# First block of the second feed-forward product: a first group cut in four, and the token tiles interleaved chunk by chunk

## The chip, the cores and the metric

The kernel runs on one core of one Trainium2 chip. The metric is the device time of the whole program in microseconds (us), lower is better. TensorE (PE in the rows) does the matrix products, VectorE (DVE) and ScalarE (ACT) the elementwise work, GpSimd (POOL) small operations and stores, SyncE (SP) issues loads.

## The reference, cut to what matters

A decoder layer with three parts, each followed by a layer norm: causal self-attention sums, a cross-attention with a bias, and a quantised feed-forward network. Only the last product of the network is touched.

```
def _L0_ffn_ref(x, W_in, b_in, W_out, b_out):
    W_in_sim = quantize_w8_per(W_in, axis=0)
    W_out_sim = quantize_w8_per(W_out, axis=1)      # one scale per row (per hidden unit)
    x_sim = quantize_a16(x)                         # one scale for the whole tensor
    hidden = jax.nn.gelu(x_sim @ W_in_sim + b_in, approximate=False)   # (8192 tokens, 2048)
    hidden_sim = quantize_a16(hidden)               # needs max |hidden| over everything
    out = hidden_sim @ W_out_sim + b_out            # (8192, 2048) @ (2048, 512)
    return out
x = _layernorm(x + ffn(x), axis=-1)
```

Because `quantize_a16` of the hidden values needs the maximum over all of them, the second product cannot begin before the first one has ended everywhere.

## The kernel before, in words

The 8192 tokens are worked in 16 blocks (`NBLK`) of 512 tokens (`BLK`), each block in four tiles of 128 tokens (t = 0..3). The 2048 hidden units are 16 chunks of 128 (`FC`, index f); four chunks are a group (`FG` = 4 groups, index g or f // 4). The first product writes its results to a table in memory; the last stage, which is the one changed, reads them back.

In this last stage one group of one block is a tile of 128 x 2048 numbers (4 chunks x 512 tokens), and it passes through five steps:

- `load_group` (SP, L1771) loads it as `hT`.
- `shift` (ACT, L1825) scales it and adds a rounding constant, into `g32`. The rows call this buffer `bt_main`, whose memory it uses.
- `scale_rows` (DVE, L1878) takes the constant off and multiplies by one number per chunk, in four instructions of 128 x 512.
- `high` (ACT, L1833) copies it to 16 bits, `g_hi`.
- `low` (DVE, L1887) writes the rest, `g_lo`. With this the group is ready for TensorE, and `lo_ready` counts it.

TensorE (`blk`, L1951) then computes for every tile t the sum over 16 chunks of two matmuls (`g_hi`, `g_lo`) each: 32 matmuls in one accumulator bank, `ps[t]`. It waits on `lo_ready` only in tile 0, at chunks 0, 4, 8 and 12, since the later tiles read the same groups. The last matmul of a tile counts `o_done`.

VectorE then finishes the tile. `residual` (L1897 to L1905) adds the residual to `ps[t]` and takes mean and variance, GpSimd computes the root (L1800), and `finish` (L1913) writes the normalised tile, which GpSimd stores.

All engines run in the order in which their instructions stand. On VectorE the order for block n is written out by hand; it works on the output tile t of block n and on group t of block n + 1 in turn:

```
for t in range(4):
    scale_rows(n + 1, t)
    residual(n, t)          # waits on o_done for tile t of block n
    low(n + 1, 1 - e, t)
    finish(n, t)            # waits for the root from GpSimd
```

Only for block 0 a prologue makes the four groups ahead of that loop. The names of the counters are `shifted` (after `shift`), `g_ready` (after `scale_rows`), `hi_ready` (after `high`) and `lo_ready` (after `low`).

Of the kernel before, what the change touches and what calls it, by code (L numbers as in the profile page):

```python
# [15 lines left out]
ALU = mybir.AluOpType  # L16
ACT = mybir.ActivationFunctionType
# [3 lines left out]
P = 128  # L21
# [1317 lines left out]
def feed_forward_stage(nc, x2_rows, w_in_rows, b_in, w_out_rows, b_out, hidden, resid, out, block, sems, shared, tail):  # L1339
# [3 lines left out]
    FC = FF // P  # L1343
    FG = FC // 4
    ROUND = 1.5 * 2.0 ** 23
# [5 lines left out]
    with ExitStack() as outer:  # L1351
# [3 lines left out]
        w2 = keep("w2", [P, FC, DIM], F16)  # L1355
        row_scale = keep("row_scale", [P, FC], F32)
# [3 lines left out]
        hT = keep("hT4", [P, FG, 4, BLK], F32)  # L1360
        hT_in = [sems.enter_context(nc.semaphore(f"hT_in{g}")) for g in range(FG)]
# [359 lines left out]
        with ExitStack() as ctx:  # L1721
# [9 lines left out]
            h_scale = sb("h_scale", [P, 1], F32)  # L1731
            o_scale = sb("o_scale", [P, 1], F32)
            minus_half = sb("minus_half4", [P, 1], F32)
            round_c = sb("round_c", [P, 1], F32)
# [5 lines left out]
            g_hi = sb("g_hi", [P, 2, FC, BLK], F16)  # L1740
            g_lo = sb("g_lo", [P, 2, FC, BLK], F16)
# [3 lines left out]
            g32 = shared.bt_main  # L1745
            ps = [ctx.enter_context(nc.psum_tensor(f"ps4{i}", [P, DIM], F32)) for i in range(4)]
# [18 lines left out]
            @block.sync  # L1765
            def _(sp):
                def load_group(n, g):
                    if not (isinstance(n, int) and n == 0):
                        sp.wait_ge(shifted, 4 * n + g - 3)
                    src = hidden[n:n + 1] if isinstance(n, int) else hidden[bass.ds(n, 1)]  # L1770
                    sp.dma_start(hT[:, g], src[:, g].rearrange("n p c t -> p (n c) t")).then_inc(hT_in[g], 16)  # L1771

                def load_row(n, t):
                    if not (isinstance(n, int) and n == 0 and t < 2):
                        sp.wait_ge(y_ready, 4 * n + t - 1)
                    src = resid[n:n + 1] if isinstance(n, int) else resid[bass.ds(n, 1)]
                    sp.dma_start(xrb[:, t % 2], src[:, :, t, :].rearrange("n p d -> p (n d)")).then_inc(xrb_in[t % 2], 16)

                for g in range(FG):
                    sp.wait_ge(h_out[g], 16 * NBLK)  # L1780
                sp.wait_ge(xres_out, 16 * NBLK)
                for g in range(FG):
                    load_group(1, g)
                    load_row(0, g)
                for n in range(1, NBLK - 1):
                    for g in range(FG):
                        load_group(n + 1, g)
                        load_row(n, g)
                for g in range(FG):
                    load_row(NBLK - 1, g)  # L1790
# [26 lines left out]
            @block.scalar  # L1817
            def _(act):
                def shift(n, g):

                    k = 4 * n + g
                    act.wait_ge(hT_in[g], 16 * (n + 1))
                    if not (isinstance(n, int) and n == 0):
                        act.wait_ge(lo_ready, k - 3)
                    act.activation(g32[:, g], hT[:, g], ACT.Identity, bias=round_c[:],  # L1825
                                   scale=h_scale[:]).then_inc(shifted, 1)

                def high(n, e, g):
                    k = 4 * n + g
                    act.wait_ge(g_ready, k + 1)  # L1830
                    if g == 0 and not (isinstance(n, int) and n < 2):
                        act.wait_ge(o_done, 4 * (n - 1))
                    act.activation(g_hi[:, e, 4 * g:4 * g + 4, :], g32[:, g], ACT.Copy).then_inc(hi_ready, 1)  # L1833

                act.wait_ge(scale_step, 3)
                act.wait_ge(round_set, 1)
                shift(0, 0)

                def blk(n, e):
                    for g in range(FG):  # L1840
                        if g < 3:
                            shift(n, g + 1)
                        elif not (isinstance(n, int) and n == NBLK - 1):
                            shift(n + 1, 0)
                        high(n, e, g)

                blk(0, 0)
                blk(1, 1)
                for m in range(1, NBLK // 2 - 1):
                    blk(2 * m, 0)  # L1850
                    blk(2 * m + 1, 1)
                blk(NBLK - 2, 0)
                blk(NBLK - 1, 1)

            @block.vector
            def _(dve):
# [16 lines left out]
                def scale_rows(n, g):  # L1873

                    k = 4 * n + g
                    dve.wait_ge(shifted, k + 1)
                    for c in range(4):
                        ins = dve.tensor_scalar(g32[:, g, c, :], g32[:, g, c, :], ROUND,  # L1878
                                                row_scale[:, 4 * g + c:4 * g + c + 1], ALU.subtract, ALU.mult)
                    ins.then_inc(g_ready, 1)  # L1880

                def low(n, e, g):
                    k = 4 * n + g
                    dve.wait_ge(hi_ready, k + 1)
                    if g == 0 and not (isinstance(n, int) and n < 2):
                        dve.wait_ge(o_done, 4 * (n - 1))
                    dve.tensor_tensor(g_lo[:, e, 4 * g:4 * g + 4, :], g32[:, g], g_hi[:, e, 4 * g:4 * g + 4, :],  # L1887
                                      ALU.subtract).then_inc(lo_ready, 1)
# [26 lines left out]

                for g in range(FG):
                    dve.wait_ge(h_out[g], 16 * NBLK)
                scale_rows(0, 0)
                for g in range(FG):
                    if g + 1 < FG:  # L1920
                        scale_rows(0, g + 1)
                    low(0, 0, g)

                def blk(n, e):
# [16 lines left out]
            @block.tensor  # L1941
            def _(pe):
                def blk(n, e):
                    for t in range(4):
                        if not (isinstance(n, int) and n == 0):
                            pe.wait_ge(y_ready, 4 * n + t - 3)
                        for f in range(FC):
                            if t == 0 and f % 4 == 0:
                                pe.wait_ge(lo_ready, 4 * n + f // 4 + 1)
                            for a, g in enumerate((g_hi, g_lo)):  # L1950
                                mm = pe.matmul(ps[t][:], g[:, e, f, t * P:(t + 1) * P], w2[:, f, :],  # L1951
                                               start=(f == 0 and a == 0), stop=(f == FC - 1 and a == 1))
                        mm.then_inc(o_done, 1)

                blk(0, 0)
                blk(1, 1)
                for m in range(1, NBLK // 2 - 1):
                    blk(2 * m, 0)
                    blk(2 * m + 1, 1)
                blk(NBLK - 2, 0)  # L1960
                blk(NBLK - 1, 1)
# [112 lines left out]
```

## Time and profile before

| | us |
|---|---|
| median of 3 runs | 2286.9 |
| lowest and highest of them | 2265.87, 2289.72 |
| the profiled execution | 2284.26 |
| its span in the trace | 2282.5 |
| TensorE busy | 2111.4 (93% of the span) |
| VectorE busy | 1735.8 (76%) |
| ScalarE busy | 1082.4 (47%) |
| granted TensorE clock, mean | 0.955 of 2.4 GHz |

Times in the rows are counted from the start of the span. The last stage begins at about 1805 us, when the first product has ended, and reaches to the end of the span. A row of the timeline gives start, duration, engine, line, operation, the tile written and the tiles read, and in brackets how long the engine had been idle and what ended that.

### The profile page before, as it was taken

The page shows a single profiled execution, that of the slowest core. Times are in us where ns is not written, and L with a number is a line of the kernel's source. Part 1 is how long each engine was busy: PE and PEld are TensorE (multiplying, and loading weights), DVE is VectorE, ACT ScalarE, POOL GpSimd, SP SyncE. Part 2 cuts the span into 40 slices and gives each one's busy share as a digit, 9 for nine tenths or more (in the row PEclk, how much of TensorE's full clock was granted, in tenths as well). Part 3 has the DMA queues.
Part 4 walks back from the last instruction along what each step waited for, and adds up shares of the span by engine and source line. Part 5 has one row for each costly group of instructions (what it writes and reads, how often), then busy time and mean ns, then how long its engine had stood idle before and what let it go on. Part 6 is the DMA issues. An engine that isn't in the chain of part 4 may idle for free.

```text
span 2282.5 us, 32943 instructions
## 1 busy us (share of the span) xinstructions
PE 2111.4 (93%) x11904; PEld 1167.9 (51%) x11904; DVE 1735.8 (76%) x3296; ACT 1082.4 (47%) x1522; POOL 822.0 (36%) x802
## 2 busy tenths in 40 slices
PE   7999999984798998999999859999999699999997
PEld 3444444431586776777777524444444344444443
DVE  6768686865677897898898656777666488888885
ACT  1444444443444555555555224444444565555551
POOL 2122221222125555556455432222222134444442
PEclk9999999996779999999999779999999899999999
DMA  6334243457749969979975437888888656666662
GB/s 233 108 126 155 94 148 110 115 137 176 188 128 208 260 166 191 279 183 208 262 181 153 136 84 267 288 288 289 267 270 272 249 195 227 224 233 230 226 226 79
DMA packets 386626, 448.46 MB, mean 196 GB/s; under 512 B 279270, under 2 KB 279430, under 8 KB 368032
## 3 DMA queue, kind: packets, MB, share of 16 engines
q1 hardware_dynamic: 322448, 286.07, 46.0%
q0 software_dynamic: 64016, 160.28, 22.9%
q8 instruction: 95, 1.56, 0.3%
q14 instruction: 67, 0.55, 0.1%
HBM read 258.93 MB, written 138.73 MB: 174 GB/s over the span
## 4 chain that ended last, share of the span: by engine, by line
PE 82%; DVE 7%; issue 6%; ACT 1%; DMA 1%; POOL 1%; SPq 0%; DVEq 0%; POOLq 0%; ACTq 0%
PE ps_h L1708 19%; PE ps L1951 19%; PE ps_proj L600 10%; PE ps_o L1275 8%; PE ps_w L1304 7%; PE ps_s L620 5%; PE ps_m L1227 3%; PE ps_o L1271 3%; PE ps_m L1229 3%; PE ps_l L1253 3%; DVE rope_t L428 1%; PE ps_t L1289 1%; PE ps_l L1250 1%; DVE x_hi L411 1%; DVE stack L1099 1%
## 5 line engine op out<-in xcount | busy, mean ns | idle before, releaser
L1708 PE MATMUL ps_h<-xT,b_rows 128*128 128x512 f16 x2048 | 444.7, 381 | 13.1 <-DMA xT<-x_lo 13.1
L1951 PE MATMUL ps<-w,g_hi 128*128 128x512 f16 x1024 | 389.3, 380 | 21.1 <-DVE g_lo L1887 21.1
L1951 PE MATMUL ps<-w,g_lo 128*128 128x512 f16 x1024 | 389.1, 380 | 0.0
L1708 PEld LDWEIGHTS ps_h<-xT,b_rows 128*128 128x128 f16 x2048 | 200.9, 98 | 256.6 <-issue 16.6
L1549 ACT ACTIVATE h<-ps_h,b_rows 128x512 f32<-128x512 f32 x256 | 199.0, 777 | 241.5 <-PE ps_h L1708 241.5
L1275 PEld LDWEIGHTS ps_o<-vm,pT 128*128 128x128 f32 x2048 | 299.2, 202 | 13.0
L1099 DVE TENSOR_REDUCE stack<-ps_m 128x2 f16<-128x308 f32 x512 | 244.2, 479 | 55.3 <-PE ps_m L1229 53.6
L1275 PE MATMUL ps_o<-vm,pT 128*128 128x33 f32 x2048 | 284.8, 265 | 0.0
L1050 ACT ACTIVATE pT<-logit 128x512 f32<-128x512 f32 x320 | 199.0, 624 | 132.3 <-DVE logit L1117 131.4
L1622 DVE TENSOR_REDUCE amax_t<-h 128x1 f32<-128x2048 f32 x64 | 146.2, 2284 | 120.8 <-ACT h L1549 120.8
L1800 POOL TENSOR_TENSOR rstd<-vare,minus_half 128x1 f32<-128x1 f32 x64 | 152.3, 2380 | 208.5 <-DVE vare L1905 208.5
L1833 ACT ACTIVATE g_hi<-bt_main 128x2048 f16<-128x2048 f32 x64 | 122.2, 1909 | 179.0 <-DVE bt_main L1878 179.0
L969 POOL TENSOR_TENSOR comb_lo<-comb,comb_hi 128x512 f16<-128x512 f32 x64 | 74.0, 1157 | 347.6 <-ACT comb_hi L1059 347.6
L1227 PE MATMUL ps_m<-kb,q_heads 128*128 128x308 f16 x512 | 161.6, 316 | 35.1 <-DVE stack L1099 15.3
L309 ACT ACTIVATE raw<-ps_proj 128x512 bf16<-128x512 f32 x128 | 76.4, 597 | 231.0 <-PE ps_proj L600 231.0
L1304 PE MATMUL ps_w<-wo_hi,combT 128*128 128x512 f16 x512 | 161.0, 398 | 24.3 <-DVE y L1145 20.8
L1117 DVE TENSOR_TENSOR logit<-ps_l,bt_main 128x512 f32<-128x512 f32 x256 | 174.0, 681 | 3.6 <-PE ps_l L1253 3.5
L1951 PEld LDWEIGHTS ps<-w,g_hi 128*128 128x128 f16 x1024 | 100.4, 98 | 144.4 <-DVE g_lo L1887 23.5
L1951 PEld LDWEIGHTS ps<-w,g_lo 128*128 128x128 f16 x1024 | 100.4, 98 | 120.8 <-issue 0.8
L1229 PE MATMUL ps_m<-b_rows,ident_h 128*128 128x308 f16 x512 | 161.3, 315 | 0.0
L1502 POOL DMA_DIRECT2D hidden<-h x64 | 35.7, 558 | 322.0 <-ACT h L1549 322.0
L1887 DVE TENSOR_TENSOR g_lo<-bt_main,g_hi 128x2048 f16<-128x2048 f32 x64 | 146.2, 2285 | 1.9 <-ACT g_hi L1833 1.5
(182 smaller groups left out, 3840.1 us busy)
## 6 DMA issues: line engine op xcount, KB each, us to landing
hidden<-h POOLq DMA_DIRECT2D x64, 1024.0 KB, 6.7
hT<-hidden SPq DMA_DIRECT2D x64, 1024.0 KB, 6.2
xc<-x_cols SPq DMA_DIRECT2D x16, 1024.0 KB, 5.1
xr<-x_rows SPq DMA_DIRECT2D x16, 1024.0 KB, 5.5
x_rows<-x POOLq DMA_DIRECT2D x16, 1024.0 KB, 4.8
x1t<-x_rows SPq DMA_DIRECT2D x64, 256.0 KB, 3.8
bt_main<-bias_main SPq DMA_DIRECT2D x16, 1024.0 KB, 6.3
xres<-x_rows SPq DMA_DIRECT2D x64, 256.0 KB, 4.1
```

Of the source, the lines that this page charges most:

```text
L600: mm = pe.matmul(ps_proj[job % 2][:], w[:, m, c, o * P:(o + 1) * P], x_[:, j % 2, c, :], start=(s == 0), stop=(s == len(terms) - 1))
L1050: act.activation(pT[:, g % 2, k, :], logit[:, (g + k) % 4], ACT.Exp, scale=SCALE).then_inc(exp_done, 1)
L1099: dve.tensor_reduce(stack[:, tile % 3, 2 * k:2 * k + 2, 3 * HD], ps_m[k % 2][:, 0:2 * KEYS].rearrange("p (h k) -> p h k", h=2), AX.X, ALU. ...
L1117: dve.tensor_tensor(logit[:, (g + k) % 4], ps_l[(5 * g + k) % 2][:], bias, ALU.add).then_inc(biased, 1)
L1227: pe.matmul(out, q_heads[:, t % 2, (k // 2) * P:(k // 2 + 1) * P], kb[:, eu, 2 * k * KEYS:(2 * k + 2) * KEYS], start=True, stop=False)
L1229: pe.matmul(out, ident_h[:], b_rows[:, t, 2 * k:2 * k + 2, :], start=False, stop=True).then_inc(mx_done, 1)
L1275: mm = pe.matmul(ps_o[c][:, base + h * VW:base + (h + 1) * VW], pT[:, g % 2, part, tok], vm[:, eu, 4 * g + h, :], start=False, stop=(part ...
L1304: mm = pe.matmul(ps_w[:], combT[:, eu, a, c, t * P:(t + 1) * P], w[:, c, :], start=(c == 0 and a == 0 and w is wo_hi), stop=(c == KC - 1 a ...
L1549: act.activation(h[:, f // 4, f % 4, :], ps_h[f % 4][:], ACT.Gelu, bias=b_in_sb[:, f:f + 1], scale=col_scale[:, f:f + 1]).then_inc(h_ready, 1)
L1708: mm = pe.matmul(ps_h[f % 4][:], w1[:, c, f * P:(f + 1) * P], xT[:, e, a, :, c, :], start=(a == 0 and c == 0), stop=(a == 1 and c == KC - 1))
L1800: pool.tensor_tensor(rstd[:, s:s + 1], vare[:, s:s + 1], minus_half[:], ALU.pow).then_inc(rstd_ready, 1)
L1951: mm = pe.matmul(ps[t][:], g[:, e, f, t * P:(t + 1) * P], w2[:, f, :], start=(f == 0 and a == 0), stop=(f == FC - 1 and a == 1))
```

## The change

The first group of block 0 passes through ScalarE and VectorE in four pieces of one chunk (128 x 512) and not as a whole. TensorE works block 0 with the chunk as its outer loop and the four token tiles as its inner one, so that each chunk is used for all four tiles before the next is taken. The counters of all later groups are shifted by three, because the first group now counts four times. The loops `blk` of all engines for blocks 1 to 15 are otherwise as they were; on VectorE this includes the loop that is quoted above for n = 0.

```
@@ SyncE, load_group
-                        sp.wait_ge(shifted, 4 * n + g - 3)
+                        sp.wait_ge(shifted, 4 * n + g)
@@ ScalarE, shift and high
-                        act.wait_ge(lo_ready, k - 3)
+                        act.wait_ge(lo_ready, k)
-                    act.wait_ge(g_ready, k + 1)
+                    act.wait_ge(g_ready, k + 4)
@@ ScalarE
-                shift(0, 0)
+                def shift_piece(c):
+                    act.activation(g32[:, 0, c], hT[:, 0, c], ACT.Identity, bias=round_c[:],
+                                   scale=h_scale[:]).then_inc(shifted, 1)
+                def high_piece(c):
+                    act.wait_ge(g_ready, c + 1)
+                    act.activation(g_hi[:, 0, c, :], g32[:, 0, c], ACT.Copy).then_inc(hi_ready, 1)
+                act.wait_ge(hT_in[0], 16)
+                shift_piece(0)
+                for c in range(4):
+                    if c < 3:
+                        shift_piece(c + 1)
+                    high_piece(c)
                 def blk(n, e):
                     for g in range(FG):
+                        if n == 0 and g == 0:
+                            shift(0, 1)
+                            continue
                         if g < 3:
                             shift(n, g + 1)
@@ VectorE, scale_rows and low
-                    dve.wait_ge(shifted, k + 1)
+                    dve.wait_ge(shifted, k + 4)
-                    dve.wait_ge(hi_ready, k + 1)
+                    dve.wait_ge(hi_ready, k + 4)
@@ VectorE
-                scale_rows(0, 0)
-                for g in range(FG):
-                    if g + 1 < FG:
-                        scale_rows(0, g + 1)
+                def scale_piece(c):
+                    dve.wait_ge(shifted, c + 1)
+                    dve.tensor_scalar(g32[:, 0, c, :], g32[:, 0, c, :], ROUND, row_scale[:, c:c + 1],
+                                      ALU.subtract, ALU.mult).then_inc(g_ready, 1)
+                def low_piece(c):
+                    dve.wait_ge(hi_ready, c + 1)
+                    dve.tensor_tensor(g_lo[:, 0, c, :], g32[:, 0, c], g_hi[:, 0, c, :], ALU.subtract).then_inc(lo_ready, 1)
+                scale_piece(0)
+                for c in range(4):
+                    if c < 3:
+                        scale_piece(c + 1)
+                    low_piece(c)
+                for g in range(1, FG):
+                    scale_rows(0, g)
                     low(0, 0, g)
@@ TensorE
-                                pe.wait_ge(lo_ready, 4 * n + f // 4 + 1)
+                                pe.wait_ge(lo_ready, 4 * n + f // 4 + 4)
-                blk(0, 0)
+                def first_blk():
+                    for f in range(FC):
+                        if f < 4:
+                            pe.wait_ge(lo_ready, f + 1)
+                        elif f % 4 == 0:
+                            pe.wait_ge(lo_ready, f // 4 + 4)
+                        for t in range(4):
+                            for a, g in enumerate((g_hi, g_lo)):
+                                mm = pe.matmul(ps[t][:], g[:, 0, f, t * P:(t + 1) * P], w2[:, f, :],
+                                               start=(f == 0 and a == 0), stop=(f == FC - 1 and a == 1))
+                            if f == FC - 1:
+                                mm.then_inc(o_done, 1)
+                first_blk()
```

On TensorE, at the beginning of block 0, the bank names change (`ps40` to `ps43` are the four tiles). Before:

```order
L1951 MATMUL ps40<-w2,g_hi 128x512 [waits lo_ready]
L1951 MATMUL ps40<-w2,g_lo 128x512
L1951 MATMUL ps40<-w2,g_hi 128x512
L1951 MATMUL ps40<-w2,g_lo 128x512
L1951 MATMUL ps40<-w2,g_hi 128x512
L1951 MATMUL ps40<-w2,g_lo 128x512
```

And in the changed kernel:

```order
L1994 MATMUL ps40<-w2,g_hi 128x512 [waits lo_ready]
L1994 MATMUL ps40<-w2,g_lo 128x512
L1994 MATMUL ps41<-w2,g_hi 128x512
L1994 MATMUL ps41<-w2,g_lo 128x512
L1994 MATMUL ps42<-w2,g_hi 128x512
L1994 MATMUL ps42<-w2,g_lo 128x512
L1994 MATMUL ps43<-w2,g_hi 128x512
L1994 MATMUL ps43<-w2,g_lo 128x512
L1994 MATMUL ps40<-w2,g_hi 128x512 [waits lo_ready]
```

A chunk now serves eight matmuls in four banks, where it served two in one. At the end of block 0 and the beginning of block 1 TensorE has, in the changed kernel:

```order
L1994 MATMUL ps40<-w2,g_hi 128x512
L1994 MATMUL ps40<-w2,g_lo 128x512
L1994 MATMUL ps41<-w2,g_hi 128x512
L1994 MATMUL ps41<-w2,g_lo 128x512
L1994 MATMUL ps42<-w2,g_hi 128x512
L1994 MATMUL ps42<-w2,g_lo 128x512
L1994 MATMUL ps43<-w2,g_hi 128x512
L1994 MATMUL ps43<-w2,g_lo 128x512
L1981 MATMUL ps40<-w2,g_hi 128x512 [waits lo_ready,y_ready4]
```

Before, the last matmul of `ps40` stood 96 matmuls ahead of that last row; now it stands 7 ahead of it. On VectorE, from the first group of block 0 to the first tile, the order before was:

```order
L1878 TENSOR_SCALAR bt_main<-bt_main,row_scale 128x512 x3
L1878 TENSOR_SCALAR bt_main<-bt_main,row_scale 128x512 [waits shifted]
L1878 TENSOR_SCALAR bt_main<-bt_main,row_scale 128x512 x3
L1887 TENSOR_TENSOR g_lo<-bt_main,g_hi 128x2048 [waits hi_ready]
L1878 TENSOR_SCALAR bt_main<-bt_main,row_scale 128x512 [waits shifted]
L1878 TENSOR_SCALAR bt_main<-bt_main,row_scale 128x512 x3
L1887 TENSOR_TENSOR g_lo<-bt_main,g_hi 128x2048 [waits hi_ready]
```

And in the changed kernel (L1938 and L1943 are the pieces):

```order
L1938 TENSOR_SCALAR bt_main<-bt_main,row_scale 128x512 [waits shifted]
L1943 TENSOR_TENSOR g_lo<-bt_main,g_hi 128x512 [waits hi_ready]
L1938 TENSOR_SCALAR bt_main<-bt_main,row_scale 128x512 [waits shifted]
L1943 TENSOR_TENSOR g_lo<-bt_main,g_hi 128x512 [waits hi_ready] x2
L1895 TENSOR_SCALAR bt_main<-bt_main,row_scale 128x512 [waits shifted]
L1895 TENSOR_SCALAR bt_main<-bt_main,row_scale 128x512 x3
L1904 TENSOR_TENSOR g_lo<-bt_main,g_hi 128x2048 [waits hi_ready]
L1895 TENSOR_SCALAR bt_main<-bt_main,row_scale 128x512 [waits shifted]
L1895 TENSOR_SCALAR bt_main<-bt_main,row_scale 128x512 x3
L1904 TENSOR_TENSOR g_lo<-bt_main,g_hi 128x2048 [waits hi_ready]
```

The scaling of a later group used to stand ahead of the `low` of the group before it; now `low` comes first, and the scaling of groups 2 and 3 stands behind it.

## Rows read from the trace of the kernel before

**Rows 1.** The page's chain that ended last, its shares by engine

```profile
PE 82%; DVE 7%; issue 6%; ACT 1%; DMA 1%; POOL 1%; SPq 0%; DVEq 0%; POOLq 0%; ACTq 0%
```

**Rows 2.** The same chain in order of time, around block 0: start, us, what

```profile
1813.98 4.08 ACT bt_main L1825 x2
...
1831.24 2.30 DVE g_lo L1887
...
1833.60 66.43 PE ps L1951 x307
```

**Rows 3.** Windows: busy us per engine, then granted clock, DMA share, GB/s

```profile
1822.20:1825.60 3.40, 3.36 (x8) 1.04 (x8) 3.40 (x5) 3.40 (x3) 0.00 (x0) 0.50 1.03 417
...
1826.00:1829.80 3.80, 2.00 (x8) 0.72 (x8) 3.75 (x5) 3.80 (x3) 0.00 (x0) 0.97 0.23 97
...
1856.00:1883.70 27.70, 27.70 (x130) 12.56 (x129) 24.47 (x45) 15.62 (x9) 12.61 (x8) 1.00 0.68 226
```

**Rows 4.** Timeline of TensorE in block 0

```profile
1822.24 0.61 PE L1951 MATMUL ps<-w,g_hi 128*128 128x512 f16 x1 [17.23 <-DVE g_lo L1887]
...
1825.20 0.63 PE L1951 MATMUL ps<-w,g_lo 128*128 128x512 f16 x1
1826.02 0.49 PE L1951 MATMUL ps<-w,g_hi 128*128 128x512 f16 x1 [0.19 <-DVE g_lo L1887]
...
1833.60 0.39 PE L1951 MATMUL ps<-w,g_hi 128*128 128x512 f16 x1 [1.89 <-DVE g_lo L1887]
...
1835.12 0.38 PE L1951 MATMUL ps<-w,g_lo 128*128 128x512 f16 x1
...
1848.93 0.38 PE L1951 MATMUL ps<-w,g_lo 128*128 128x512 f16 x1
```

**Rows 5.** Timeline of ScalarE in block 0

```profile
1817.96 1.89 ACT L1833 ACTIVATE g_hi<-bt_main 128x2048 f16<-128x2048 f32 x1
1819.76 2.08 ACT L1825 ACTIVATE bt_main<-hT,round_c,h_scale 128x2048 f32<-128x2048 f32 x1
1821.75 1.89 ACT L1833 ACTIVATE g_hi<-bt_main 128x2048 f16<-128x2048 f32 x1
```

**Rows 6.** Timeline of VectorE: output tiles 0 and 3 of block 0

```profile
1835.53 0.75 DVE L1897 SCALAR_TENSOR_TENSOR y<-ps,o_scale,xrb 128x512 f32<-128x512 f32 x1 [0.41 <-PE ps L1951]
...
1837.34 2.28 DVE L1887 TENSOR_TENSOR g_lo<-bt_main,g_hi 128x2048 f16<-128x2048 f32 x1
...
1856.25 0.75 DVE L1897 SCALAR_TENSOR_TENSOR y<-ps,o_scale,xrb 128x512 f32<-128x512 f32 x1 [0.23 <-PE ps L1951]
...
1858.06 2.28 DVE L1887 TENSOR_TENSOR g_lo<-bt_main,g_hi 128x2048 f16<-128x2048 f32 x1
...
1861.26 1.67 DVE L1878 TENSOR_SCALAR bt_main<-bt_main,row_scale 128x512 f32<-128x512 f32 x4
1863.16 0.75 DVE L1897 SCALAR_TENSOR_TENSOR y<-ps,o_scale,xrb 128x512 f32<-128x512 f32 x1 [0.23 <-PE ps L1951]
```

**Rows 7.** Groups by shape with 128x512 operands: count, busy us, mean ns

```profile
L1549 ACT ACTIVATE h<-ps_h,b_rows 128x512 f32<-128x512 f32 x256 | 199.0, 777 | 241.5 <-PE ps_h L1708 241.5
L1059 ACT ACTIVATE comb_hi<-comb 128x512 f16<-128x512 f32 x64 | 39.3, 614 | 6.2 <-DVE comb L1132 6.2
L1117 DVE TENSOR_TENSOR logit<-ps_l,bt_main 128x512 f32<-128x512 f32 x256 | 174.0, 681 | 3.6 <-PE ps_l L1253 3.5
L1878 DVE TENSOR_SCALAR bt_main<-bt_main,row_scale 128x512 f32<-128x512 f32 x256 | 106.9, 480 | 1.9 <-ACT bt_main L1825 1.9
```

**Rows 8.** Windows around two waits of TensorE in the cross-attention stage

```profile
732.70:735.30 2.60, 0.01 (x1) 0.00 (x0) 0.76 (x2) 1.54 (x2) 0.18 (x1) 1.00 1.03 395
...
888.00:893.36 5.36, 0.01 (x2) 0.03 (x2) 0.81 (x2) 1.54 (x2) 1.32 (x2) 0.78 1.41 246
893.36:895.00 1.64, 1.62 (x4) 0.38 (x5) 1.56 (x6) 0.00 (x0) 0.00 (x0) 0.50 1.75 193
...
897.00:899.00 2.00, 2.00 (x12) 1.49 (x11) 1.87 (x4) 1.08 (x3) 0.00 (x0) 0.79 1.31 96
```

## The prediction

> **What bounds the kernel now.** I read the chain of work that ended last first. TensorE holds 82% of it [rows 1], and in the last stage it is the only link from 1833.60 us on [rows 2]. The windows then say what a full stretch of that stage looks like: from 1856.00 to 1883.70 TensorE is busy all of 27.70 us at a granted clock of 1.00, which is the higher level, 2.4 GHz, with VectorE busy 24.47 us beside it [rows 3]. So a later block is bound by TensorE, with VectorE close behind. The beginning of the stage is the exception: ScalarE and VectorE prepare the first groups while TensorE waits, 17.23 us before its first matmul and 1.89 us before the last of the four groups [rows 4].
>
> From the timeline of TensorE come two durations. At the higher level 71 matmuls lie between the starts 1833.60 and 1848.93, which makes 0.216 us each, so 1.73 for the 8 matmuls that tile 0 has for one group and 6.91 for the 32 of a tile. At the lower level (1.2 GHz, 0.50 in [rows 3]) the first eight start 0.423 us apart, 1822.24 to 1825.20 [rows 4]. After 1833.60 tile 0 has 8 matmuls left and the other tiles 96. Block 0 thus ends at 1833.60 + 104 x 0.216 = 1856.06, and block 1, with 128, at 1883.71, if nothing waits. Nothing does [rows 3].
>
> **Part 1, the four pieces.** The trace has no such pieces, so I take the nearest 128x512 shapes: 0.78 us for ScalarE with bias and scale, 0.61 for its copy, 0.68 for a VectorE subtraction, 0.48 for the scaling by a chunk's number [rows 7]. ScalarE's next instruction starts about 0.09 before the one ahead ends (1.89 long, next after 1.80; 2.08 long, next after 1.99) [rows 5]. From ScalarE's start at 1813.98 [rows 2]: first shift to 1814.76, second to 1815.45, first copy (the first scaling, to 1815.3, is done) to 1815.97, first subtraction to about 1816.7. TensorE's first matmul is then at 1816.8, where it was at 1822.24: 5.4 us earlier.
>
> The price is on ScalarE. Four shifts and four copies take 4 x (0.69 + 0.52) = 4.84 us, where one of each took 1.99 + 1.80 = 3.79. Moreover the second group's shift no longer stands ahead of the first group's copy. ScalarE comes to it at 1818.9 (the fourth copy waits for a scaling), ends it at 1821.0 and the third group's at 1823.0. The scaling of group 1 ends at 1822.7, its copy at 1824.8, its subtraction at 1827.1. The scaling of group 2 now stands behind that subtraction, so a group costs 1.67 + 1.91 + 2.28 = 5.86 in series: groups 2 and 3 are ready at about 1833 and 1839.
>
> The Trainium skill ("VectorE: DVE Perf Modes", section on the TRN2 errata) speaks against such pieces: instructions on on-chip memory pay a fixed part each. The rows show it at the size used above, and by an estimate from the page's ScalarE figure the six added instructions would cost 1.1 us, against the 1.05 above, so the sum would be the same.
>
> **Part 2, four tiles per chunk.** A chunk now feeds 8 matmuls and a group 32, 6.91 us, more than the 5.86 that the next group needs. So TensorE starts at 1816.8, runs 3.8 us (9 matmuls) at the lower level as it did before, does the other 23 of the group to 1825.5, waits to 1827.15 for group 1, and then does 96 without a wait: 1827.15 + 20.74 = 1847.9. Group 2 is wanted at 1834.1 and group 3 at 1841.0, so these have 1 and 2 us to spare. **Block 0 ends 8.2 us earlier.** Bounds: with group 1 there in time 1846.2 (9.9 earlier); with group 1 a further microsecond late 7.2.
>
> **Part 3, what stands behind block 0.** This is what decides. VectorE's loop for block 0 is unchanged: scaling of group t of block 1, residual of tile t of block 0, `low` of group t of block 1, `finish` of tile t. Before, tile 0 was complete at 1835.5, and during tiles 1 to 3 VectorE had 20 us in which it could make `low` of block 1, one group per tile; the last ended at 1858.06 + 2.28 = 1860.34 and was wanted at 1856.06 + 24 x 0.216 = 1861.24 [rows 6]. It was made just in time. Now all four tiles end together: `ps40` ends 7 matmuls before the end of the block. Behind the residual of tile 0, on VectorE, stands everything that block 1 needs, and TensorE waits for it at once, since its tile 0 wants all four groups.
>
> Working: the last matmul of tile 0 starts at 1847.9 - 7 x 0.216 = 1846.4. The residual starts 0.41 later (1835.12 to 1835.53 [rows 4, 6]), `low` 1.81 after it, and takes 2.28 [rows 6], and TensorE starts 0.06 behind its end (1831.24 + 2.30 to 1833.60 [rows 2]): 1846.8 + 1.81 + 2.28 + 0.06 = 1850.95. **That is a wait of 3.05 us.** Then each further group costs VectorE a whole turn of its loop. A turn is 1863.16 - 1856.25 = 6.91 us, 0.23 of it waiting for TensorE [rows 6], so 6.68 when the tiles are there; in it TensorE has only 8 matmuls, 1.73. Three turns are three waits of 4.95, **14.85 us**. Group 3 of block 1 reaches TensorE at 1850.95 + 20.04 = 1871.0, and the block ends at 1871.0 + 22.46 = 1893.5, where it ended at 1883.7: **9.7 us later**. Nothing gives this back, since from there on TensorE is the bound.
>
> ScalarE's copies of block 1 lie beside the residuals (1.91 in 1.81) and add 0.1 at most per turn. Loads: `hT` of group 3 of block 1 stands on SyncE behind a load that waits for the first residual; it is used two turns later. Both cost nothing, and with a short turn that cover would go.
>
> **The clock.** After a wait of 2.6 us the clock was still at 1.00. In one of 5.36 us it fell (mean 0.78), then stood at 0.50 with TensorE busy to about 897.8, 4.5 us [rows 8]. At the beginning of the stage it was low for 3.8 us [rows 3, 4]. The waits of 4.95 lie nearer to the 5.36. In the first groups the lower level hides in the waits (3.4 us of work in a turn of 6.68). Behind the last one it counts, half of 3.8 to 4.5 us: **2.0 us**. Bounds: 0, if the bursts keep the level or raise it before the last, and 4.4, if it lasts twice as long.
>
> The Trainium skill ("TensorE: Matmul & The Clock Gate", section "HAM oscillation — how this bites in real kernels") has the case of bursts with waits between them, each of which starts at the lower clock. By it the term stands as taken; without it the sum would be 2.0 less.
>
> **The sum.** -8.2 + 3.05 + 14.85 + 2.0 = +11.7 us. Against the profiled execution, 2284.26 (span 2282.5 and 1.8 around it), that makes 2296.0. The median shown is 2.6 above that execution, so I forecast 2286.9 + 11.7 = 2298.6. About 1% (22.9 us) is what a measurement of this kernel can tell from no change: its three runs lie 24 us apart.
>
> **Rivals.**
>
> A, not slower: the wait in block 1 doesn't come, and block 0's gain stays: 2286.9 - 8.2 = 2278.7. The Trainium skill ("Perfetto Trace Analysis", section on optimizing Scalar/DVE operations) has it so: breaking up instructions may let waiting engines go on sooner, which holds of part 1. It decides at the turn L for which 3.05 + 3 x (L - 1.73) = 8.2, L = 3.4 us. Against it: scaling, residual's first instruction and `low` alone are 1.67 + 0.75 + 2.28 = 4.70 [rows 6]. Chance 0.05.
>
> B, slower by over 1%: the clock stays low behind the last wait. At 0.423 - 0.216 = 0.207 us for each matmul, it takes 64 matmuls at the lower level (22.9 - 9.7 = 13.2) to pass the bound; all 104 would give 2286.9 + 9.7 + 21.5 = 2318. Against it: in both places the clock rose after 3.8 to 4.5 us of work [rows 4, 8]. Chance 0.05.
>
> C, the change doesn't do what it says in block 0: ScalarE and VectorE are later by over 2 us per group than worked out, and TensorE waits for groups 2 and 3 as before. The gain goes, the wait of block 1 stays: up to +19.9, 2306.8. Against it: 5.86 against 6.91 per group. Chance 0.06.
>
> D, VectorE stays behind: after group 3 it comes 2.6 to the residual of tile 0 of block 1, which TensorE has ended after 2.0, so it is 0.6 behind. It gains 0.23 a tile, and `low` of the next block has 0.9 to spare, so I count nothing. If that isn't so, a few more waits come, 1 to 4 us: 2299.6 to 2302.6. Chance 0.10.
>
> The forecast has 0.74. The range, 2276 to 2309, takes in A, C and D and the bounds of the terms, and at its lower end a median out of runs such as the lowest one (2265.87 + 11.7 = 2277.6). Slower by over 1% needs 2309.8: B and, by the scatter of the runs, some of C and of the forecast, 0.13. Faster by over 1% needs less than 2264: 0.03. Within 1%: 0.84.
>
> **What would show it.** First matmul of block 0 near 1816.8, one wait of about 1.7 before its group 1, end near 1848. Then waits of TensorE on VectorE's `low`: one of 3 and three of about 5 us (less by 1.7 where the clock is at 0.50), 24 matmuls of tile 0 of block 1 spread over 20 us, and from block 2 on no wait. VectorE has no idle time ahead of the residuals of tiles 1 to 3 of block 0. The prediction is wrong if the turn is much shorter than 6.7, or if block 1's groups are ready ahead of the first residual.

## The result

The changed kernel takes 2288.86 us in the median of 20 runs, the kernel before 2277.86 in 20. The ratio is 1.0049, with a 95% interval of 1.0027 to 1.0072: slower by about 11 us, which is less than the 1% bound and clear of zero. One of the 20 runs of the kernel before took 2766 us; the ratio leaves it out. Forecast were +11.7 us. The median itself lies 9.7 below the forecast one, since that was counted from 2286.9, and the median of the kernel before came out 9.0 lower with more runs.

The profiled execution of the changed kernel has a span of 2282.6 us, the one before 2282.5. That doesn't contradict the ratio. The two executions differ ahead of the change: the last stage of the changed one happened to begin 10.8 us earlier, and its first product had already begun 10.6 us earlier (1349.72 against 1360.28). So I measure the **length of the last stage**, from ScalarE's first shift to the end of the span. It is 2282.5 - 1813.98 = 468.5 us before [rows 2] and 2282.6 - 1803.15 = 479.45 after, **+10.9**. All times called "after the shift" below count from that first shift.

The chain of the changed kernel in order of time (start, us, what). It answers to [rows 2]:

```profile
1803.15 1.52 ACT bt_main L1839 x2
...
1814.17 2.30 DVE g_lo L1904
...
1816.52 19.61 PE ps L1994 x90
1836.15 0.76 DVE y L1914
...
1838.20 2.51 POOL rstd L1800
...
1841.19 1.74 DVE bt_main L1895 x4
1842.96 1.92 ACT g_hi L1833
...
1857.52 2.30 DVE g_lo L1904
1859.82 0.05 issue
1859.87 40.33 PE ps L1981 x179
```

Before, TensorE held the chain from 1833.60, 19.6 us after the shift, to the end. Now it holds it from 1816.52, loses it at 1836.15 to VectorE, GpSimd and ScalarE for three turns of a loop, and has it back for good only at 1859.87, 56.7 us after the shift.

TensorE's timeline: the rows at which a wait ends, and the first row behind the last wait that is at the higher clock level again. They answer to [rows 4]:

```profile
1806.03 0.61 PE L1994 MATMUL ps<-w,g_hi 128*128 128x512 f16 x1 [11.83 <-DVE g_lo L1943]
...
1816.52 0.39 PE L1994 MATMUL ps<-w,g_hi 128*128 128x512 f16 x1 [0.58 <-DVE g_lo L1904]
...
1840.38 0.38 PE L1981 MATMUL ps<-w,g_hi 128*128 128x512 f16 x1 [2.98 <-DVE g_lo L1904]
...
1847.25 0.61 PE L1981 MATMUL ps<-w,g_hi 128*128 128x512 f16 x1 [4.98 <-DVE g_lo L1904]
...
1853.56 0.61 PE L1981 MATMUL ps<-w,g_hi 128*128 128x512 f16 x1 [2.72 <-DVE g_lo L1904]
...
1859.87 0.61 PE L1981 MATMUL ps<-w,g_hi 128*128 128x512 f16 x1 [2.71 <-DVE g_lo L1904]
...
1863.13 0.38 PE L1981 MATMUL ps<-w,g_hi 128*128 128x512 f16 x1
```

Block 0 has 96 matmuls from 1816.52 on and ends at 1837.26, 34.1 after the shift (42.1 before): 8.0 us gained. Block 1 then has 3.12 us to its first matmul and turns of 6.87, 6.31 and 6.31 us with 8 matmuls each. From 1863.13 it runs 96 without a wait to 1883.87, 80.7 after the shift (69.7 before): 11.0 us lost. The stage's +10.9 is all there; later blocks give nothing back and cost nothing.

VectorE's timeline shows the loop that sets these turns. It answers to [rows 6]:

```profile
1836.15 0.75 DVE L1914 SCALAR_TENSOR_TENSOR y<-ps,o_scale,xrb 128x512 f32<-128x512 f32 x1 [6.40 <-PE ps L1994]
...
1837.96 2.28 DVE L1904 TENSOR_TENSOR g_lo<-bt_main,g_hi 128x2048 f16<-128x2048 f32 x1
1840.73 0.55 DVE L1930 TENSOR_SCALAR o<-y,mv,rstd 128x512 f32<-128x512 f32 x1 [0.49 <-POOL rstd L1800]
1841.19 1.73 DVE L1895 TENSOR_SCALAR bt_main<-bt_main,row_scale 128x512 f32<-128x512 f32 x4
1842.85 0.74 DVE L1914 SCALAR_TENSOR_TENSOR y<-ps,o_scale,xrb 128x512 f32<-128x512 f32 x1
...
1844.90 2.29 DVE L1904 TENSOR_TENSOR g_lo<-bt_main,g_hi 128x2048 f16<-128x2048 f32 x1 [0.18 <-ACT g_hi L1833]
1847.11 0.54 DVE L1930 TENSOR_SCALAR o<-y,mv,rstd 128x512 f32<-128x512 f32 x1
```

VectorE stood idle 6.40 us ahead of the first residual, waiting for the end of block 0, with the groups of block 1 behind it in its queue. After that it is idle only for 0.49 us (the root) and 0.18 us (ScalarE's copy) in the first turn, and for 0.18 us in each of the next two.

Windows of the changed kernel (busy per engine, granted clock, DMA share, GB/s), to be set against [rows 3, 8]:

```profile
1837.30:1840.38 3.08, 0.11 (x1) 0.03 (x1) 2.86 (x5) 0.00 (x0) 2.18 (x1) 1.00 0.82 192
1840.38:1842.10 1.72, 1.72 (x8) 0.68 (x8) 1.37 (x4) 0.00 (x0) 0.84 (x2) 1.00 0.93 391
1842.10:1847.25 5.15, 0.17 (x1) 0.01 (x1) 4.86 (x9) 3.90 (x2) 0.79 (x2) 0.87 0.66 191
1847.25:1850.60 3.35, 3.35 (x8) 1.03 (x8) 3.32 (x7) 1.33 (x1) 0.62 (x1) 0.50 0.67 269
...
1862.80:1890.00 27.20, 27.20 (x127) 12.37 (x126) 23.70 (x43) 14.67 (x8) 12.61 (x8) 1.00 0.63 218
```

The wait of 3 us left the clock up, the one of 5 let it fall. The second, third and fourth bursts ran at 0.50, and 8 matmuls of the fourth cost 1.5 us more than at the higher level.

### The profile page after: what moved, and what is told of

Read it like the earlier page. It is cut to its first block, busy times and chain, and to the rows that moved or that the text cites. A ratio compares the mean times of both kernels' runs of the same rounds, so it can differ in the third digit from the quotient of the medians.

```text
span 2282.6 us, 32952 instructions
## 1 busy us (share of the span) xinstructions
PE 2113.2 (93%) x11904; PEld 1165.6 (51%) x11904; DVE 1734.8 (76%) x3299; ACT 1083.9 (47%) x1528; POOL 822.5 (36%) x802
## 4 chain that ended last, share of the span: by engine, by line
PE 82%; DVE 7%; issue 5%; ACT 2%; DMA 1%; POOL 1%; SPq 0%; DVEq 0%; POOLq 0%; ACTq 0%
PE ps_h L1708 19%; PE ps L1981 18%; PE ps_proj L600 10%; PE ps_o L1275 8%; PE ps_w L1304 7%; PE ps_s L620 5%; PE ps_m L1227 3%; PE ps_o L1271 3%; PE ps_m L1229 3%; PE ps_l L1253 3%; DVE rope_t L428 1%; PE ps_t L1289 1%; PE ps L1994 1%; PE ps_l L1250 1%; DVE x_hi L411 1%
## 5 line engine op out<-in xcount | busy, mean ns | idle before, releaser
L1981 PE MATMUL ps<-w,g_hi 128*128 128x512 f16 x960 | 366.8, 382 | 13.4 <-DVE g_lo L1904 13.4
L1981 PE MATMUL ps<-w,g_lo 128*128 128x512 f16 x960 | 366.7, 382 | 0.0
L1981 PEld LDWEIGHTS ps<-w,g_hi 128*128 128x128 f16 x960 | 94.5, 98 | 130.5 <-DVE g_lo L1904 12.7
L1981 PEld LDWEIGHTS ps<-w,g_lo 128*128 128x128 f16 x960 | 94.5, 98 | 114.2 <-issue 2.5
```

## The experiments

The table gives the stage length by the trace, and the timed ratio to the kernel before where there is one. Where the clock behaves alike, the stage length repeats within 0.1 us (479.45 and 479.4 for the changed kernel); the kernel before has one profile.

| | stage, us | against before | timed ratio (95% interval) |
|---|---|---|---|
| before | 468.5 | | |
| changed | 479.45 | +10.9 | 1.0049 (1.0027 to 1.0072) |
| e1 pieces only | 475.6 | +7.1 | 1.0047 (1.0012 to 1.0082) |
| e2 chunks only | 483.0 | +14.5 | 1.0125 (1.0086 to 1.0163) |
| e3 changed, filler in the waits | 478.0 | +9.5 | |
| e4 changed, block 1's groups first | 472.1 | +3.6 | 1.0054 (1.0022 to 1.0087) |
| e5 tiles in pairs | 472.1 | +3.6 | 1.0034 (1.0004 to 1.0064) |
| e6 as e4, lighter block 0 | 472.1 | +3.6 | |
| e7 changed, prologue pipelined | 480.9 | +12.4 | |
| e8 as e4, earlier loads | 471.4 | +2.9 | |
| e9 as e8, lighter block 0 | 468.6 | +0.1 | |
| e10 as e8, finishes put off | 470.85 | +2.3 | 1.0005 (0.9979 to 1.0031) |
| e11 changed, again | 479.4 | +10.9 | |
| e12 as e7, again | 479.5 | +10.9 | |

In e2 and e4 the timed ratios say more than the stage: about 28 and 12 us, with intervals that begin at 20 and 5 us, against 14.5 and 3.6. These are 4 and 10 runs whose earlier stages scatter too. Where the difference comes from isn't shown, and the text below rests on the stage.

**e1, one half alone: the pieces.** In the changed kernel TensorE's first block gets its old loop order:

```
 def first_blk():
-    for f in range(FC):
-        ... waits on lo_ready at f
-        for t in range(4):
+    for t in range(4):
+        for f in range(FC):
+            ... the same waits, at t == 0
```

> The four pieces alone; TensorE works block 0 tile by tile as before. The measure is the length of the last stage, from ScalarE's first shift to the end of the span: 468.5 us before, 479.5 in the changed kernel. Theory (the waits stand in block 1, because all four tiles of block 0 end together): they don't come here, since tile 0 ends 20 us before the block. But tile 0 wants all four groups at once, and group 3 is ready 25.0 us after the first shift (it was 19.6), so block 0 ends at 25.1 + 22.5 = 47.6 where it was 42.1: stage +5.5 us, no wait in block 1. Rival (the pieces and the serial prologue are the whole loss): the stage is 11 us longer here as well. Rival (only the tile order matters): +0.

Measured: +7.1. No wait in block 1. Group 3 of block 0 reaches TensorE 25.06 after the shift, where it did at 19.62: +5.4. The rest is the clock, which I had not put in: the waits in tile 0 became longer (6.15, 2.26 and 2.56 us), it fell, and 8 matmuls behind the last one cost 1.7 us. The row of that last wait is

```profile
1828.08 0.39 PE L1993 MATMUL ps<-w,g_hi 128*128 128x512 f16 x1 [2.56 <-DVE g_lo L1904]
```

So this half alone is a loss, and in another way than the changed kernel: group 3 is late. Under the old order this is on the path, under the new one it is not. The pieces themselves are the smaller part of the delay. e7 has the pieces with the old prologue, and there group 3 is ready 20.9 us after the shift, 1.3 later than in the kernel before (19.6). The other 4.1 us belong to the serial prologue that e1 kept.

**e2, the other half: four tiles per chunk.** The kernel before, with TensorE's `blk(0, 0)` replaced:

```
-                blk(0, 0)
+                for f in range(FC):
+                    if f % 4 == 0:
+                        pe.wait_ge(lo_ready, f // 4 + 1)
+                    for t in range(4):
+                        ... two matmuls into ps[t]
```

> Four tiles per chunk in block 0 alone, without the pieces and with the old prologue. Theory: TensorE starts 8.3 us after the first shift, has the first group's 32 matmuls done at about 18 (13 of them at the lower clock level) and block 0 at 38.5, 3.6 us earlier than before; then the same waits come as in the changed kernel, 3 + 5 + 2.7 + 2.7 us of it seen at either clock level, block 1 takes 46.6 us in place of 27.65 (+19.0): stage +15 us, so this half alone is slower than both halves together. Rival (pieces are the loss): stage shorter than before, -3.6.

Measured: +14.5. TensorE has the same four waits, 2.98, 4.98, 2.72 and 2.71 us, only 3.6 us later than in the changed kernel. The two rows at the head of block 1:

```profile
1858.25 0.38 PE L1951 MATMUL ps<-w,g_hi 128*128 128x512 f16 x1 [2.98 <-DVE g_lo L1887]
1865.12 0.61 PE L1951 MATMUL ps<-w,g_hi 128*128 128x512 f16 x1 [4.98 <-DVE g_lo L1887]
```

The loss comes with this half. With it, the pieces are worth 3.6 us, since TensorE can use an early chunk at once. Block 0 ended 37.7 us after the shift and not at the expected 38.5, with 9 matmuls at the lower clock level and not 13.

**e3, the price of the clock.** In the changed kernel, for block 1, tile 0:

```
+                                if isinstance(n, int) and n == 1 and f > 0:
+                                    for _ in range(18):
+                                        pe.matmul(ps_fill[:], w2[:, 0, 0:P], w2[:, 0, :], start=True, stop=True)
                                 pe.wait_ge(lo_ready, 4 * n + f // 4 + 4)
```

> The changed kernel with 18 matmuls into a spare bank ahead of each of the three later groups of tile 0 of block 1, in the time that TensorE waits there (18 x 0.216 = 3.9 us in a wait of 5). They are work that the result doesn't use. This prices the clock alone: the granted clock should stay at 1.00 through block 1, and the 7 to 8 matmuls that ran 0.21 us longer behind the last wait should run at 0.216: stage 1.5 us shorter than the 479.5 of the changed kernel, with VectorE's turns as they are. If the clock term is nothing: no difference. If TensorE's loads or the filler slow VectorE: longer.

Measured: 1.5 us shorter than the changed kernel. The groups reach TensorE at the same times to 0.02 us, and the clock stays up through the whole of tile 0:

```profile
1854.00:1874.00 20.00, 17.61 (x80) 7.53 (x81) 18.64 (x35) 11.90 (x6) 4.22 (x7) 1.00 0.72 251
```

Of the 10.9 us, 1.5 are the clock, and 9.4 the waits for VectorE less what block 0 gained.

**e4, another order on VectorE.** In the changed kernel, VectorE's block 0:

```
-                blk(0, 0)
+                scale_rows(1, 0)
+                scale_rows(1, 1)
+                low(1, 1, 0)
+                scale_rows(1, 2)
+                low(1, 1, 1)
+                residual(0, 0)
+                scale_rows(1, 3)
+                low(1, 1, 2)
+                finish(0, 0)
+                low(1, 1, 3)
+                for t in range(1, 4):
+                    residual(0, t)
+                    finish(0, t)
```

On SyncE groups 3 of block 1 and 0 of block 2 are loaded ahead of the rows for tiles 2 and 3, and the prologue on VectorE is that of the kernel before, as in e7.

> The changed kernel with VectorE's block 0 loop written in another order: the first two groups of block 1 are made before the residual of tile 0, the last two before the residual of tile 1, with the loads that these need issued earlier, and the scaling of groups 2 and 3 of block 0 ahead of the subtraction before it. Theory A (only the order of this one loop is wrong): the waits of block 1 shrink from 13.4 to about 3 us and nothing comes in their place: stage 8 to 11 us shorter than in the changed kernel, at or below the 468.5 of before. Theory B (VectorE has no slack in any block, so what is put off comes due in the next one): the waits of block 1 shrink as in A, but the residuals and finishes of tiles 1 to 3 now stand behind them, and TensorE waits some 10 to 12 us for the groups of block 2: stage about 6 us longer than before, 4 to 5 shorter than in the changed kernel.

Measured: +3.6, and neither theory in full. The waits of block 1 shrink to 1.02 and 0.76 us. In block 2 two new ones come:

```profile
1877.00 0.61 PE L2002 MATMUL ps<-w,g_hi 128*128 128x512 f16 x1 [3.18 <-DVE g_lo L1911]
1883.31 0.61 PE L2002 MATMUL ps<-w,g_hi 128*128 128x512 f16 x1 [3.08 <-DVE g_lo L1911]
```

That is what theory B says in kind, but 6.3 us in place of 10 to 12: the three finishes in a row cost less than a turn each. Behind VectorE stood something else too, on ScalarE:

```profile
1858.10 2.10 ACT L1832 ACTIVATE bt_main<-hT,round_c,h_scale 128x2048 f32<-128x2048 f32 x1 [13.33 <-DMA hT<-hidden]
```

The load of group 1 of block 2 stood on SyncE behind rows that wait for residuals. VectorE lost 1.87 us behind it.

**e5, a middle way.** The kernel before, with block 0 in pairs of tiles on TensorE:

```
-                blk(0, 0)
+                for pair in ((0, 1), (2, 3)):
+                    for f in range(FC):
+                        ... wait on lo_ready at f % 4 == 0 of the first pair
+                        for t in pair:
+                            ... two matmuls into ps[t]
```

> The kernel before with block 0 worked chunk by chunk for tiles 0 and 1 and then for tiles 2 and 3 (no pieces). TensorE has 16 matmuls per group (3.5 us) while ScalarE delivers one per 3.8, so block 0 ends about 5 us earlier than before, at 37 us after the first shift. Tiles 0 and 1 are complete at about 24, so VectorE can go on. Theory B: TensorE's lead is worth nothing, since VectorE's loop sets when group 3 of block 1 is ready (47.3 us as before): the 5 us come back as waits in block 1, stage 468.5 +- 1. Theory A: stage 4 to 5 us shorter than before.

Measured: +3.6, where I expected none. TensorE did come to block 1 ahead of VectorE, and the lead came back as one wait of 4.96 us for its last group:

```profile
1855.23 0.61 PE L1951 MATMUL ps<-w,g_hi 128*128 128x512 f16 x1 [4.96 <-DVE g_lo L1887]
```

That is 48.6 us after the shift. The 47.3 of my expectation was when TensorE took this group in the kernel before; ready it was at 46.4 (1858.06 + 2.28 + 0.06 [rows 6]). So it came 2.2 us later than before, and 1.4 of these cost time. The first residual is 2.3 later (23.8, before 21.6), since tile 0 ends with tile 1, and VectorE waits once more for tile 2, which ends with tile 3:

```profile
1844.23 0.75 DVE L1897 SCALAR_TENSOR_TENSOR y<-ps,o_scale,xrb 128x512 f32<-128x512 f32 x1 [0.73 <-PE ps L1962]
```

The clock fell in the wait of 4.96 us and 11 matmuls behind it ran at the lower level, 2.3 us. Theory B holds in kind. Its size left out both, the 1.4 and the 2.3.

**e6, less work for VectorE.** As e4, with `bn_stats` and `bn_aggr` of block 0 replaced by two memsets, so that block 0 is left without its mean and variance and only the time is of use:

> As e4, and the mean and variance of the four tiles of block 0 left out on VectorE (replaced by constants, 0.7 to 0.9 us less per tile, so about 3.4 us less work). Theory B (VectorE's total work is what TensorE waits for in block 2): the stage is about 3.5 us shorter than in e4, with the waits of block 2 shorter by as much. Theory A: no difference from e4, since its waits would not be there.

Measured: as long as e4 (472.07 and 472.14). Taken alone this speaks for theory A. The trace shows why it doesn't: VectorE came 2.8 us earlier to block 2 and stood there, waiting for ScalarE, which waited for the load:

```profile
1854.20 2.29 DVE L1911 TENSOR_TENSOR g_lo<-bt_main,g_hi 128x2048 f16<-128x2048 f32 x1 [4.44 <-ACT g_hi L1840]
...
1850.28 2.09 ACT L1832 ACTIVATE bt_main<-hT,round_c,h_scale 128x2048 f32<-128x2048 f32 x1 [13.82 <-DMA hT<-hidden]
```

The test was spoilt by my own order of loads, so e8 and e9 repeat it without that.

**e7, the serial prologue.** In the changed kernel `scale_rows(0, g + 1)` stands ahead of `low(0, 0, g)` again.

> The changed kernel with the prologue of block 0 on VectorE as it was before: the scaling of groups 2 and 3 ahead of the subtraction of the group before. Groups 2 and 3 get ready about 2 and 4 us earlier, but TensorE didn't wait for them. Theory (all is set by the end of block 0 on TensorE): only the 0.6 us wait for group 1 can change, stage 479.5 to 478.9. Rival (the serial prologue costs): 2 to 4 us shorter.

Measured: 1.5 us longer than the changed kernel, as neither said. The waits are the same to 0.01 us except the one of group 1. Group 3 of block 0 is ready 4.1 us earlier, as expected, and TensorE doesn't want it so early. Its `low` here, from 18.59 us after the shift, and in the changed kernel, from 22.73:

```profile
1835.17 2.29 DVE L1904 TENSOR_TENSOR g_lo<-bt_main,g_hi 128x2048 f16<-128x2048 f32 x1 [1.50 <-ACT g_hi L1833]
```

```profile
1825.88 2.29 DVE L1904 TENSOR_TENSOR g_lo<-bt_main,g_hi 128x2048 f16<-128x2048 f32 x1 [1.98 <-ACT g_hi L1833]
```

The difference of 1.5 us is the number of matmuls at the lower level behind the last wait (low matmuls below): 14 here, 8 there. Windows from the last wait on, of this kernel and of its repetition e12, both 6.70 us:

```profile
1873.30:1880.00 6.70, 6.70 (x18) 2.49 (x19) 4.94 (x11) 3.90 (x2) 1.71 (x2) 0.55 0.50 163
```

```profile
1881.80:1888.50 6.70, 6.70 (x25) 2.75 (x26) 5.13 (x11) 3.89 (x2) 1.93 (x2) 0.77 0.51 161
```

**e11 and e12, the same two kernels again.**

> The changed kernel once more, unaltered. In its first profile 8 matmuls behind the last wait of block 1 ran at the lower clock level (1.5 us); in the kernel with the pipelined prologue it were 14 (2.9 us), with the same waits to 0.01 us. If that difference is of the execution and not of the kernel, this profile shows the same waits (3.0, 5.0, 2.7, 2.7 us) and a number of low matmuls between 7 and 16, and a stage of 479.4 to 481.

> The kernel with the pipelined prologue once more. As for e11: the waits as in its first profile, the low matmuls behind the last of them 7 to 16, stage 479.4 to 481. If the prologue's order costs the 1.5 us, it shows 14 and 480.9 again.

Measured: 479.4 and 479.5, with 7 and 8 low matmuls. So the 1.5 us of e7 belong to that execution: the same kernel had 14 once and 8 once. The order of the prologue is worth nothing here, which the theory had said.

**e8, e4 with earlier loads.**

```
                 load_group(1, 3)
-                load_group(2, 0)
+                for g in range(FG):
+                    load_group(2, g)
                 load_row(0, 2)
```

> As e4, with the loads of all four groups of block 2 issued ahead of the rows that tiles 2 and 3 of block 0 need. In e4 ScalarE stood idle 13.3 us for such a load and VectorE 1.87 us behind it before its first group of block 2; VectorE's own backlog may be what limits behind that. Theory (VectorE's backlog): its low of group 0 of block 2 starts at about 54.0 us after the first shift (55.7 in e4), three turns of 6.31 follow, group 3 reaches TensorE at 75.3, where it stood at 74.9 in the kernel before: stage 468.9 and 1.5 to 2.9 of the lower clock level, 470.4 to 471.8, against 472.1 in e4. Rival (in e4 only the loads were the bound): the waits of block 2 go away and the stage is 465 or less, below the kernel before.

Measured: 471.4. The `low` of the first group of block 2 starts 54.0 after the shift, and the last group reaches TensorE at 75.27, as worked out from VectorE's backlog. The waits of block 2 didn't go away; they are 1.50 and 4.41 us:

```profile
1853.38 2.29 DVE L1912 TENSOR_TENSOR g_lo<-bt_main,g_hi 128x2048 f16<-128x2048 f32 x1 [0.18 <-ACT g_hi L1841]
```

```profile
1874.66 0.61 PE L2003 MATMUL ps<-w,g_hi 128*128 128x512 f16 x1 [4.41 <-DVE g_lo L1912]
```

**e9, the same with the lighter block 0.**

> As e8, with the mean and variance of block 0's four tiles left out on VectorE (constants in their place). In e6 the loads hid this. Theory (VectorE's backlog): it comes 2.8 us earlier to block 2, group 3 at about 72.5 in place of 75.3: stage 2.8 us shorter than in e8 or more, if the clock doesn't fall, so 466 to 467.6. Rival: as long as e8.

Measured: 468.6, 2.8 less than e8. That this equals the forecast is partly luck. The last group of block 2 came at 73.32, only 1.95 earlier (2.8 were expected), and 0.9 is fewer low matmuls, 8 in place of 12. The missing 0.84 is a wait that the lighter work brought out. The last finish of block 0 stands 1.53 us for the store that still reads its half of `o`, where in e8 it stood 0.69 for the root:

```profile
1851.24 0.55 DVE L1943 TENSOR_SCALAR o<-y,mv,rstd 128x512 f32<-128x512 f32 x1 [1.53 <-DMA out<-o]
```

So with the loads out of the way, work taken off VectorE comes back as time, less what another wait takes up, and the arrival of the last group moves with it:

```profile
1876.62 0.39 PE L2008 MATMUL ps<-w,g_hi 128*128 128x512 f16 x1 [4.41 <-DVE g_lo L1912]
```

**e10, finishes put off.** As e8, with `finish(0, t - 1)` behind `residual(0, t)`.

> As e8, with each finish of block 0 behind the residual of the next tile, so that VectorE doesn't stand 0.69 us for GpSimd's root three times but once. Theory: 1.4 us less in VectorE's backlog, stage 469 to 470.4, level with the kernel before within 2 us (0.1%), so the timed ratio is 1.000 +- what it can tell. It is the nearest of these orders to the kernel before; if it is shorter than 468.5, TensorE's lead is worth something after all.

Measured: 470.85, and the last group at 75.50, no earlier than in e8. The waits of the finishes didn't vanish. GpSimd's queue has root 0, store 0, root 1, store 1, and each store waits for its finish, so a finish put off holds back the next root. VectorE's last two finishes:

```profile
1848.71 0.55 DVE L1938 TENSOR_SCALAR o<-y,mv,rstd 128x512 f32<-128x512 f32 x1 [0.44 <-DMA out<-o]
1850.76 0.55 DVE L1938 TENSOR_SCALAR o<-y,mv,rstd 128x512 f32<-128x512 f32 x1 [1.50 <-POOL rstd L1808]
```

Together 1.94 us, 0.44 for a store and 1.50 for a root, against 3 x 0.69 in e8. By the timed ratio this is level with the kernel before (1.0005); no order tried was measurably faster than it.

## Why the prediction was right

*The wait behind block 0.* Right, and the decisive step. All four tiles end together, VectorE stands idle 6.40 us with block 1's groups queued behind a residual, and TensorE waits four times. e2 shows that the interleaved tiles bring it. e4 shows that VectorE's order places it: with the groups of block 1 first, these waits go from 13.4 to 1.8 us.

*Sizes.* First matmul 2.8 after the shift, measured 2.88. End of block 0 33.9, measured 34.1, so 8.0 gained in place of 8.2. First gap to block 1 3.05, measured 3.12. Three turns 20.04, measured 6.87 + 6.31 + 6.31 = 19.49. Clock 2.0, measured 1.5. With the measured numbers the sum is -8.0 + 3.12 + 5.14 + 2 x 4.58 + 1.5 = +10.9, where 5.14 and 4.58 are the turns less the 1.73 of 8 matmuls. No term is off by more than 0.6 us.

*The turn.* This was the term with a wrong reason in it. I took the turn with its wait for GpSimd's root, as it stood in every row of before. From group 1 of block 1 on `low` started 0.18 us later, since it waited for ScalarE's copy, and behind that there was no wait for the root. The prediction had that copy as a cost of 0.1 per turn; with it the turn was 6.31 and not 6.68. The first turn had both waits, 0.49 and 0.18, and took 6.87. The last section has the rows.

*The wait for group 1 of block 0.* Forecast 1.7, measured 0.58. Group 1 came at 13.37 (forecast 13.2), but the lower clock level had lasted for 14 matmuls and not 9, so TensorE was later too. The two cancel, as the slower matmuls hid in the wait.

*Rivals.* A (not slower): it decided at a turn of 3.4 us, measured 6.31 and more. B (clock): 8 matmuls at the lower level behind the last wait, at most 14, where 64 were needed. C: groups 2 and 3 were ready at 19.2 and 25.0, before TensorE wanted them. D: no wait from block 2 on. VectorE was not behind at all: it waited 1.48 us for TensorE ahead of the residual of tile 0 of block 1, because the low clock made TensorE the later one. In e3, where the clock stays up, that residual (1875.67) has no wait, so the two engines come out level and not 0.6 apart.

What the prediction didn't say, and the experiments add, is that a better order alone doesn't bring the 8 us. e5 and e8 give TensorE a lead in block 0 and get it back as a wait for VectorE one block on; e9 shows, for the second of them, that the waits of block 2 shorten with VectorE's work (from 5.9 to 4.7 us). That VectorE's total work forbids any gain isn't shown: other orders, or another place for its work, weren't tried.

## What to carry to other kernels

When the inner and outer loops of a producer are exchanged, look at what its results release. Here the first block ended 8 us earlier, but its four tiles ended together, and the engine behind it, which had spread its work over the gaps between them, had it all to do at once while the next block waited. An engine that is 0.2 us per tile from being the bound can't make up a lead or a backlog of several microseconds: ask what it does in the time that is removed. And where an earlier stage varies by 10 us from run to run, measure the stage that was changed from its own beginning.

## What the runs showed of the hardware

In VectorE's loop GpSimd's root, one operation on 128 x 1 numbers, takes 2.5 us or 0.56, by whether it starts ahead of VectorE's `low` (0.56) or while that runs (2.5). The first three of the changed kernel:

```profile
1838.20 2.50 POOL L1800 TENSOR_TENSOR rstd<-vare,minus_half 128x1 f32<-128x1 f32 x1 [35.23 <-DVE vare L1922]
...
1844.81 0.56 POOL L1800 TENSOR_TENSOR rstd<-vare,minus_half 128x1 f32<-128x1 f32 x1 [2.49 <-DVE vare L1922]
...
1851.12 0.56 POOL L1800 TENSOR_TENSOR rstd<-vare,minus_half 128x1 f32<-128x1 f32 x1 [2.56 <-DVE vare L1922]
```

In the first case `low` had begun 0.24 us earlier, at 1837.96, and the root ended 0.46 after it. In the second `low` began 0.09 us after the root had started, and took 2.29 us as ever. So a `low` that starts 0.2 us later shortens the turn by 0.37. The rows show this order and these durations; why the root takes longer beside a `low` that is already running isn't shown.

The clock: in the changed kernel the wait of 2.98 us left it up and the one of 4.98 let it fall, as did that of 4.96 in e5. The length of the wait alone doesn't decide it. In e10 TensorE had run at the higher level for the whole stretch ahead of a wait of 2.19 us (granted clock 1.00 from 1862.00 to 1867.60), and came out of it at the lower one:

```profile
1869.84 0.61 PE L2003 MATMUL ps<-w,g_hi 128*128 128x512 f16 x1 [2.19 <-DVE g_lo L1912]
```

In e9, behind a wait of 4.41, the first matmul still ran at the higher level (0.39), and 8 matmuls from 0.23 us later on ran at the lower one. In e8, behind a wait of the same 4.41, the first was already at the lower level (0.61). So the fall can come after the work has begun again. The number of low matmuls behind the last wait of block 1 was 8 and 7 (the changed kernel, e11), and 14 and 8 (e7, e12), with equal waits in all four.
